# Issuing the packed keys' eight transfers from ScalarE instead of the SP queue

## The chip, the cores and the metric

The kernel runs on one core of one Trainium2 chip. The metric is the device time of one execution in microseconds (us), as the median of several runs. Beside it stands one profiled execution, whose trace is read here.

## The reference

The input x has 8 sequences of 2048 tokens with 256 features. One transformer layer is computed:

```
def attention(x):                       # 16 heads of 16
    k = q = heads(tanh(x))
    static = tanh(x) @ W.T
    v = heads(static)
    # per head, token by token:
    #   S = lam * S;  u = beta * (v_t - S^T k_t);  S += k_t u^T;  o_t = S^T q_t
    return layernorm(static + o) * gamma + beta_ln
x = layernorm(x + attention(x))
h = silu(x @ Wg.T) * (x @ Wu.T)         # 768 hidden features
return layernorm(x + h @ Wd.T)
```

The recurrence is sequential over the 2048 tokens, and the kernel works it in chunks.

## The kernel before, in words

The tokens are cut into 32 blocks of 64 tokens (8 sequences x 64 tokens), and each block into 4 chunks of 16 tokens, in which 8 x 16 = 128 rows fill the partitions. Within a chunk the recurrence becomes products with the chunk's gram matrix (keys by keys) and the inverse of a triangular matrix made from it. From chunk to chunk only the state S goes on.

The work is software-pipelined over steps numbered s. In step s the recurrence runs for block s, while block s+1 has its gram matrix and inverse computed, block s+2 has its input loaded, passed through tanh and transposed, and the two blocks behind go through the norms and the dense layers (gate, up, down). `p` is the parity of s. Each engine has a hand-written order of instructions for one step (`act_step`, `dve_step`, `pe_step`, `pool_step`, `sp_step`), and the engines are tied together by counting semaphores; `n_of(name, q)` is the count that stands for "block q is done". An engine's instructions start in their written order, so a wait holds back all that is behind it.

All transfers are issued by the queue of SyncE, the SP queue (`sp_step`, L1093). In one step its order is: `kb` part 0 (8 issues, L1073), the two stores of the transposed keys `xt` to `scr_x` in DRAM (L1004), the packed keys `xb` (8 issues, L1026), the block-diagonal keys `E` (8 issues, L1017; the profile names them `e`), the first store of the inverse (L1048), the residual (4 issues, L1083), the second store of the inverse (L1048), `tb` part 0 (8 issues, L1060), `kb` part 1 (8 issues), the gram matrix out to DRAM and back in head-major order (L1034, L1041), `tb` part 1 (8 issues), the next block's x (4 issues, L995) and the output (4 issues, L1091). Both `xb` and `E` are read from `scr_x`: the first packed, the second with each sequence's 16x16 pieces on a diagonal. TensorE multiplies them in `pe_gram` (L216) in the next step.

What ScalarE does around the place of the change, in `act_step`: the update of chunk 3 (L664), x1's high half 0 (L772), the decay (L673), x1's high half 1 (L772), the SiLU of gate tile 0 (`act_hidden`, L778), the scaled keys `k16` part 0 (L699), the high half of the inverse part 0 (`act_store_inverse`, L730), the product's high half (L784), gate tile 1 (L778) and the state's high half (L668). VectorE's order there is: 14 rounds of the inverse (L443, L451), `dve_multiply` for gate tile 0 (L495), the low half of the inverse part 0 (L458), the state (L388, L393, L399), and later, at the head of the next step, the low half of the inverse part 1 (L458 again).

Two more waits bear on the order: tanh of the next block (L677) waits for the load of x, and `act_static_out` (L706) waits for the output of an earlier block to have left its buffer.

Of the kernel before, what the change touches and what calls it, by code (L numbers as in the profile page):

```python
# [13 lines left out]
B, L, D = 8, 2048, 256  # L14
H, DH = 16, 16
# [20 lines left out]
def build(nc, x, W, ln_gamma, ln_beta, eta, lam_logit, w_gate, w_up, w_down, out):  # L36
# [3 lines left out]
    with ctx:  # L40
        def sb(name, shape, dt=F32):
            return ctx.enter_context(nc.sbuf_tensor(name, shape, dt))

        def sem(name):
            return ctx.enter_context(nc.semaphore(name))
# [28 lines left out]
        xb = sb("xb", [P, 2, H, C, NW], F16)  # L74
# [43 lines left out]
        scr_x = nc.dram_tensor("scr_x", [2, 2, P, B, T], F16).ap()  # L118
# [6 lines left out]
            xtd=32, e=128, xb=128, vp=2, v=2,  # L125
            gp=4, ga=4, g=4, gd=16, gh=16,
# [11 lines left out]
        SEM = {name: sem("s_" + name) for name in PER}  # L138
# [7 lines left out]
        s_hop = sem("s_hop")  # L146
# [6 lines left out]
        def n_of(name, q, k=None):  # L153

            k = PER[name] if k is None else k
            if k <= 0:
                q, k = q - 1, k + PER[name]
            return q * PER[name] + k if q >= 0 else 0
# [8 lines left out]
        def live(q):  # L167
            return 0 <= q < NS

        def later(q):  # L170
            return 1 <= q < NS
# [512 lines left out]
        def act_transpose_keys(act, q, p, half):  # L684
            src = pf[half][:, :].rearrange("p (n t) -> p t n", n=NW)
            dst = xt[:, half].rearrange("p z b i n -> p z (b i) n")
            act.wait_ge(SEM["xtp"], n_of("xtp", q, half + 1))
            if half == 0:
                act.wait_ge(SEM["vp"], n_of("vp", q - 1))
                act.wait_ge(SEM["xtd"], n_of("xtd", q - 1))  # L690
            act.activation(dst[:, 0], src, ACT.Copy, scale=KS).then_inc(SEM["xth"], 1)
# [75 lines left out]
        def act_transpose_x1(act, q, p, half):  # L767
            act.wait_ge(SEM["x1p"], n_of("x1p", q, half + 1))
            if half == 0:
                act.wait_ge(SEM["gt"], n_of("gt", q - 1))  # L770
                act.wait_ge(SEM["gu"], n_of("gu", q - 1))
            act.activation(x1hi[:, half, :], pg[half][:, :], ACT.Copy, scale=XS).then_inc(SEM["x1h"], 1)  # L772

        def act_hidden(act, q, p, t):
            k = t % 2
            act.wait_ge(SEM["gt"], n_of("gt", q, t + 1))
            act.wait_ge(SEM["hl"], n_of("hl", q, t - 1))
            act.activation(gate[:, k, :], pg[k][:, :], ACT.Silu, scale=W_SCALE / XS).then_inc(SEM["si"], 1)  # L778

        def act_multiply(act, q, p, t):  # L780
# [2 lines left out]
                act.wait_ge(SEM["dn"], n_of("dn", q - 1))  # L783
            act.activation(hhi[:, t, :], gate[:, t % 2, :], ACT.Copy).then_inc(SEM["hh"], 1)  # L784

        def act_step(act, s, p):
            if live(s):
                act_store_inverse(act, s, p, 1)
# [98 lines left out]
                act_decay(act, s, p, 3)  # L887
            if live(s - 1):
                act_transpose_x1(act, s - 1, 1 - p, 1)
                act_hidden(act, s - 1, 1 - p, 0)  # L890
            if live(s + 2):
                act_scale_keys(act, s + 2, p, 0)
# [104 lines left out]
        def sp_store_keys(sp, q, p, half):  # L997
            sp.wait_ge(SEM["xt"], n_of("xt", q, half + 1))
            sp.sem_inc(s_hop, 1)
            if half == 0:  # L1000
                sp.wait_ge(SEM["e"], n_of("e", q - 1))
                sp.sem_inc(s_hop, 1)
                sp.wait_ge(SEM["xb"], n_of("xb", q - 1))
            sp.dma_start(scr_x[:, half].rearrange("z p b t -> p z (b t)"),  # L1004
                         xt[:, half].rearrange("p z b i n -> p z (b i n)")).then_inc(SEM["xtd"], 16)
# [11 lines left out]
                sp.dma_start(E[p][DH * b:DH * (b + 1), :, :, b].rearrange("k z h i n -> k (z h) (i n)"),  # L1017
                             src[:, :, b, :]).then_inc(SEM["e"], 16)

        def sp_spread_packed_keys(sp, q, p):  # L1020
            src = scr_x.rearrange("z f (h k) b t -> k (z f h) b t", k=DH)
            sp.wait_ge(SEM["gp"], n_of("gp", q - 1))
            sp.sem_inc(s_hop, 1)
            sp.wait_ge(SEM["xtd"], n_of("xtd", q))
            for b in range(B):
                sp.dma_start(xb[DH * b:DH * (b + 1)].rearrange("k z h i n -> k (z h) (i n)"),  # L1026
                             src[:, :, b, :]).then_inc(SEM["xb"], 16)

        def sp_store_gram(sp, q, p):
            sp.wait_ge(SEM["g"], n_of("g", q))  # L1030
            sp.sem_inc(s_hop, 1)
            sp.wait_ge(SEM["gh"], n_of("gh", q - 1))

            sp.dma_start(scr_g.rearrange("h b i t -> (b i) h t"),  # L1034
                         gs[:, :, :, :].rearrange("p h j n -> p h (j n)")).then_inc(SEM["gd"], 16)
# [27 lines left out]
        def sp_load_kb(sp, q, p, g):  # L1063
            if q == 0:

                sp.wait_ge(s_pool0, 14)
                sp.sem_inc(s_hop, 1)
            sp.wait_ge(SEM["k16"], n_of("k16", q, g + 1))
            sp.sem_inc(s_hop, 1)
            sp.wait_ge(SEM["sp"], n_of("sp", q - 1, 2 * g + 2))  # L1070
            for b in range(B):
                rows = slice(C * b, C * (b + 1))
                sp.dma_start(kb[rows, g, :, b].rearrange("i h k z m -> i h (k z m)"),  # L1073
                             k16[rows, g].rearrange("i h k z m -> i h (k z m)")).then_inc(SEM[f"kb{g}"], 16)
# [18 lines left out]
        def sp_step(sp, s, p):  # L1093
            if live(s + 1):
                sp_load_kb(sp, s + 1, 1 - p, 0)
            if later(s + 2):
                sp_store_keys(sp, s + 2, p, 0)
                sp_store_keys(sp, s + 2, p, 1)
                sp_spread_packed_keys(sp, s + 2, p)
                sp_spread_keys(sp, s + 2, p)  # L1100
            if live(s + 1):
                sp_store_inverse(sp, s + 1, 1 - p, 0)
            if live(s):
                sp_load_residual(sp, s, p)
            if live(s + 1):
                sp_store_inverse(sp, s + 1, 1 - p, 1)
                sp_load_inverse(sp, s + 1, 1 - p, 0)
                sp_load_kb(sp, s + 1, 1 - p, 1)
            if live(s + 2):
                sp_store_gram(sp, s + 2, p)  # L1110
                sp_load_gram(sp, s + 2, p)
            if live(s + 1):
                sp_load_inverse(sp, s + 1, 1 - p, 1)
            if later(s + 3):
                sp_load_x(sp, s + 3, 1 - p)
            if live(s - 1):
                sp_store_out(sp, s - 1, 1 - p)


        def all_steps(eng, step):  # L1120
            for s in range(FIRST, LAST):
                step(eng, s, s % 2)
# [26 lines left out]
        @block.sync  # L1149
        def _(eng):  # L1150
            bc = lambda a, n: a.rearrange("(o n) -> o n", o=1).to_broadcast([P, n])
            sp_load_x(eng, 0, 0)
            eng.dma_start(sc[:, ETA:ETA + 1], eta.to_broadcast([P, 1])).then_inc(s_ldc, 16)
            eng.dma_start(sc[:, LOGIT:LOGIT + 1], lam_logit.to_broadcast([P, 1])).then_inc(s_ldc, 16)
            eng.dma_start(w_nat, W.rearrange("(a p) d -> p a d", p=P)).then_inc(s_ldw, 16)
            eng.dma_start(wg_nat, w_gate.rearrange("(t p) d -> p t d", p=P)).then_inc(s_ldn, 16)
            eng.dma_start(wu_nat, w_up.rearrange("(t p) d -> p t d", p=P)).then_inc(s_ldn, 16)
            for a in range(2):
                eng.dma_start(wd_nat[a], w_down[a * P:(a + 1) * P, :]).then_inc(s_ldn, 16)
            eng.dma_start(gamma[:, :], bc(ln_gamma, D)).then_inc(s_ldb, 16)  # L1160
            eng.dma_start(lnb[:, :], bc(ln_beta, D)).then_inc(s_ldb, 16)

            eng.wait_ge(s_pool0, 10)
            sp_store_keys(eng, 0, 0, 0)
            sp_store_keys(eng, 0, 0, 1)
            sp_spread_packed_keys(eng, 0, 0)
            sp_spread_keys(eng, 0, 0)
            all_steps(eng, sp_step)
            eng.wait_ge(SEM["out"], NS * PER["out"])
# [26 lines left out]
        @block.scalar  # L1196
        def _(eng):
            eng.wait_ge(s_ldc, 32)
            eng.activation(sc[:, OML:OML + 1], sc[:, LOGIT:LOGIT + 1], ACT.Sigmoid, scale=-1.0).then_inc(s_a0, 1)
            act_activate(eng, 0, 0)  # L1200
            act_transpose_keys(eng, 0, 0, 0)
            act_transpose_keys(eng, 0, 0, 1)
            for j, (_, dst) in enumerate(jobs):
                eng.wait_ge(s_ps, j + 1)
                eng.activation(dst, ps[j % 2], ACT.Copy).then_inc(s_wt, 1)
            eng.wait_ge(s_c, N_SETUP)
            all_steps(eng, act_step)
# [96 lines left out]
```

## Time and profile before

| | |
|---|---|
| Time, median of 3 runs | 1717.36 us |
| Lowest and highest | 1714.75 and 1728.76 us |
| Profiled execution: time | 1734.76 us |
| Profiled execution: span of the core | 1733.0 us |
| Mean granted TensorE clock (share of full speed) | 0.872 |
| Busy: TensorE, VectorE, ScalarE, GpSimd | 1373.0, 1359.0, 1118.9, 839.5 us |

The busy times are summed over the span of the one profiled execution. The SP queue is not counted as an engine in that table; its issues are seen in the timeline of the queue. In the timelines PE is TensorE, DVE VectorE, ACT ScalarE, POOL GpSimd, and SPq the queue of SyncE.

### The profile page before, as it was taken

Reading aid. Unit: us, or ns where it says so; the run is one execution under the profiler, and the core shown is the slowest. Engines: PE = TensorE matmul, PEld = TensorE weight load, DVE = VectorE, ACT = ScalarE, POOL = GpSimd, SP = SyncE. Lnnn points to the kernel's source line nnn. Section 1 sums busy time; section 2 is a strip of 40 time slices with the busy share of each in tenths; the row PEclk is TensorE's granted clock in tenths of the full one; section 3 lists DMA queues with packets and bytes.
Section 4 is the critical chain, followed back from the end, with each engine's and each line's share of the span. In section 5 each row is a group of like instructions: output and inputs, shape, how many; then the busy total and the mean of one; then the engine's idle time right before and its main releaser. Section 6 shows DMA issues by size and latency. Waiting matters only on the chain.

```text
span 1733.0 us, 53678 instructions
## 1 busy us (share of the span) xinstructions
PE 1373.0 (79%) x21032; PEld 1070.7 (62%) x21032; DVE 1359.0 (78%) x3461; ACT 1118.9 (65%) x2357; POOL 839.5 (48%) x1106
## 2 busy tenths in 40 slices
PE   4358778888887888878888888888888878888765
PEld 3346666666666666666666666666666666666532
DVE  4578888888888788888888888888888888888731
ACT  3336667666766767666776666766766666776543
POOL 6024455445444545444455554444555444455542
PEclk9558989888988999888999998989998898898866
DMA  4555544555554555555555665654555655555200
GB/s 119 116 106 119 111 114 114 117 118 111 130 111 116 113 123 117 117 119 118 116 121 118 118 121 112 124 116 114 123 120 108 115 119 117 116 120 109 57 13 25
DMA packets 701325, 190.98 MB, mean 110 GB/s; under 512 B 620944, under 2 KB 688528, under 8 KB 701072
## 3 DMA queue, kind: packets, MB, share of 16 engines
q1 hardware_dynamic: 701072, 187.56, 50.3%
q8 instruction: 165, 2.70, 0.7%
q14 instruction: 88, 0.72, 0.1%
HBM read 103.55 MB, written 67.11 MB: 98 GB/s over the span
## 4 chain that ended last, share of the span: by engine, by line
DVE 24%; SPq 22%; DMA 16%; PE 15%; issue 11%; ACT 8%; POOL 3%; ACTq 0%; POOLq 0%; DVEq 0%
SPq L1060 9%; DMA scr_g<-gs 6%; DMA xa<-L_attn_x 6%; PE pg L253 4%; SPq L1073 4%; PE pc L182 4%; DVE tt L451 4%; PE pu L253 4%; SPq L995 3%; DVE gs L443 3%; DVE gate L495 2%; DVE xt L406 2%; DVE x1lo L488 2%; DMA y_out<-v 2%; DVE U L382 2%
## 5 line engine op out<-in xcount | busy, mean ns | idle before, releaser
L954 POOL TENSOR_TENSOR hlo<-gate,hhi 128x512 f16<-128x512 f32 x192 | 263.7, 1383 | 377.3 <-ACT hhi L784 375.4
L182 PE MATMUL pc<-R,tb 128*128 128x32 f16 x4096 | 158.2, 186 | 128.1 <-DVE R L372 125.2
L182 PEld LDWEIGHTS pc<-R,tb 128*128 128x128 f16 x4096 | 146.7, 118 | 148.9 <-DVE R L372 145.7
L182 PE MATMUL pc<-U,kb 128*128 128x32 f16 x4096 | 158.9, 188 | 95.4 <-DVE U L382 95.3
L182 PEld LDWEIGHTS pc<-U,kb 128*128 128x128 f16 x4096 | 146.9, 118 | 124.7 <-DVE U L382 124.6
L182 PEld LDWEIGHTS pc<-S,e 128*128 128x128 f16 x4096 | 151.9, 118 | 61.7 <-DVE S L399 55.9
L182 PE MATMUL pc<-S,e 128*128 128x32 f16 x4096 | 157.3, 186 | 38.8 <-DVE S L399 38.7
L279 PE MATMUL pd<-wd_t,hhi 128*128 128x256 f16 x768 | 178.2, 278 | 7.9 <-POOL hlo L954 5.6
L279 PE MATMUL pd<-wd_t,hlo 128*128 128x256 f16 x768 | 178.0, 278 | 0.0
L216 PEld LDWEIGHTS pf<-xb,e 128*128 128x128 f16 x4096 | 153.6, 118 | 32.9 <-DMA e<-scr_x 17.6
L216 PE MATMUL pf<-xb,e 128*128 128x32 f16 x4096 | 156.2, 191 | 18.5 <-DMA e<-scr_x 16.9
L495 DVE SCALAR_TENSOR_TENSOR gate<-pu,gate 128x512 f32<-128x512 f32 x192 | 128.9, 685 | 49.9 <-ACT gate L778 34.9
L253 PE MATMUL pg<-x1hi,wg_t 128*128 128x512 f16 x384 | 155.0, 404 | 11.4 <-DVE x1lo L488 9.9
L443 DVE TENSOR_TENSOR gs<-tt,gh 128x56 f32<-128x56 f32 (+6 forms) x448 | 145.2, 324 | 23.6 <-ACT tt L720 14.6
L778 ACT ACTIVATE gate<-pg 128x512 f32<-128x512 f32 x192 | 114.0, 594 | 76.7 <-PE pg L253 73.7
L451 DVE TENSOR_TENSOR tt<-tt,gs 128x56 f32<-128x56 f32 (+6 forms) x448 | 152.3, 340 | 12.1
L253 PE MATMUL pg<-x1lo,wg_t 128*128 128x512 f16 x384 | 153.1, 399 | 0.0
L784 ACT ACTIVATE hhi<-gate 128x512 f16<-128x512 f32 x192 | 119.7, 629 | 50.4 <-DVE gate L495 49.0
L253 PE MATMUL pu<-x1hi,wu_t 128*128 128x512 f16 x384 | 149.1, 388 | 0.3 <-DVE gate L495 0.3
L253 PE MATMUL pu<-x1lo,wu_t 128*128 128x512 f16 x384 | 149.1, 388 | 0.0
L227 PE MATMUL pf<-w_t,xt 128*128 128x256 f16 x1024 | 140.1, 283 | 0.4 <-DVE gs L434 0.4
L434 DVE SCALAR_TENSOR_TENSOR gs<-pf,gs 128x256 f32<-128x256 f32 x128 | 84.9, 663 | 64.5 <-ACT gs L714 64.5
(134 smaller groups left out, 3229.0 us busy)
## 6 DMA issues: line engine op xcount, KB each, us to landing
xa<-L_attn_x SPq DMA_DIRECT2D x128, 128.0 KB
scr_x<-xt SPq DMA_DIRECT2D x64, 256.0 KB, 2.1
xb<-scr_x SPq DMA_DIRECT2D x256, 64.0 KB, 2.8
e<-scr_x SPq DMA_DIRECT2D x256, 64.0 KB, 3.5
scr_g<-gs SPq DMA_DIRECT2D x32, 512.0 KB, 3.5
gh<-scr_g SPq DMA_DIRECT2D x32, 512.0 KB, 3.4
kb<-k SPq DMA_DIRECT2D x512, 32.0 KB, 2.2
scr_t<-t SPq DMA_DIRECT2D x64, 256.0 KB, 3.5
```

The source lines that it names most:

```text
L182: last = pe.matmul(pc2[:, :, cols], stationary(h, a), moving[:, :, cols], start=a == 0, stop=a == 1)
L216: last = pe.matmul(pf[n % 2][:, 2 * h * C:2 * (h + 1) * C].rearrange("p (z j) -> p z j", z=2), E[p][:, ez, h, :, :, n].rearrange("p b i -> ...
L227: last = pe.matmul(pf[g][:, (n % 2) * D:(n % 2 + 1) * D], xt[:, half, xz, :, :, n].rearrange("p b i -> p (b i)"), w_t[:, half, wz, :], sta ...
L253: last = pe.matmul(bank[:, :], wt[:, half, t * P:(t + 1) * P], xp[:, half, :], start=half + part == 0, stop=half + part == 2)
L279: last = pe.matmul(pd[:, (n % 2) * D:(n % 2 + 1) * D], hp[:, t, n * P:(n + 1) * P], wd_t[:, t, :], start=n % 2 + t + part == 0, stop=n % 2 ...
L443: dve.tensor_tensor(tmp[:, m, 0:C - 1 - j, :], tt[:, m, j:j + 1, :].to_broadcast([P, j, C - 1 - j, NW]), gh[:, i, j, :][:, None].to_broadc ...
L451: dve.tensor_tensor(tt[:, m, i, :], tt[:, m, i, :], tmp[:, m, 0:C - 1 - j, :], ALU.add)\
L495: dve.scalar_tensor_tensor(gate[:, k, :], pu[k][:, :], W_SCALE * HS / XS, gate[:, k, :], ALU.mult, ALU.mult).then_inc(SEM["h"], 1)
L778: act.activation(gate[:, k, :], pg[k][:, :], ACT.Silu, scale=W_SCALE / XS).then_inc(SEM["si"], 1)
L784: act.activation(hhi[:, t, :], gate[:, t % 2, :], ACT.Copy).then_inc(SEM["hh"], 1)
L954: pool.tensor_tensor(hlo[:, t, :], gate[:, t % 2, :], hhi[:, t, :], ALU.subtract).then_inc(SEM["hl"], 1)
L1060: sp.dma_start(tb[C * b:C * (b + 1), g, :, b].rearrange("j h i z m -> j h (i z m)"), scr_t[g, :, b].rearrange("h j t -> j h t")).then_inc( ...
```

## The change

The eight issues of the packed keys leave the SP queue, together with the two waits ahead of them (`gp`: the gram products of the block before are done; `xtd`: the keys have landed in DRAM). The same eight issues, with the same two waits, now stand in ScalarE's order, behind x1's high half 1 and ahead of the SiLU of gate tile 0. For block 0 they stand in ScalarE's set-up, behind the two transposed keys. Transfers, sizes, counts and semaphores stay as they are.

```
+        def act_spread_packed_keys(act, q, p):
+            src = scr_x.rearrange("z f (h k) b t -> k (z f h) b t", k=DH)
+            act.wait_ge(SEM["gp"], n_of("gp", q - 1))
+            act.wait_ge(SEM["xtd"], n_of("xtd", q))
+            for b in range(B):
+                act.dma_start(xb[DH * b:DH * (b + 1)].rearrange("k z h i n -> k (z h) (i n)"),
+                              src[:, :, b, :]).then_inc(SEM["xb"], 16)
...
             if live(s - 1):
                 act_transpose_x1(act, s - 1, 1 - p, 1)
+            if later(s + 2):
+                act_spread_packed_keys(act, s + 2, p)
+            if live(s - 1):
                 act_hidden(act, s - 1, 1 - p, 0)
...
-        def sp_spread_packed_keys(sp, q, p):
-            src = scr_x.rearrange("z f (h k) b t -> k (z f h) b t", k=DH)
-            sp.wait_ge(SEM["gp"], n_of("gp", q - 1))
-            sp.sem_inc(s_hop, 1)
-            sp.wait_ge(SEM["xtd"], n_of("xtd", q))
-            for b in range(B):
-                sp.dma_start(xb[DH * b:DH * (b + 1)].rearrange("k z h i n -> k (z h) (i n)"),
-                             src[:, :, b, :]).then_inc(SEM["xb"], 16)
...
             if later(s + 2):
                 sp_store_keys(sp, s + 2, p, 0)
                 sp_store_keys(sp, s + 2, p, 1)
-                sp_spread_packed_keys(sp, s + 2, p)
                 sp_spread_keys(sp, s + 2, p)
...
             sp_store_keys(eng, 0, 0, 1)
-            sp_spread_packed_keys(eng, 0, 0)
             sp_spread_keys(eng, 0, 0)
...
             act_transpose_keys(eng, 0, 0, 1)
+            act_spread_packed_keys(eng, 0, 0)
             for j, (_, dst) in enumerate(jobs):
```

## Rows read from the trace of the kernel before

**Rows 1.** The page: busy time, and the chain of waits by engine and line.

```profile
PE 1373.0 (79%) x21032; PEld 1070.7 (62%) x21032; DVE 1359.0 (78%) x3461; ACT 1118.9 (65%) x2357; POOL 839.5 (48%) x1106
...
DVE 24%; SPq 22%; DMA 16%; PE 15%; issue 11%; ACT 8%; POOL 3%; ACTq 0%; POOLq 0%; DVEq 0%
SPq L1060 9%; DMA scr_g<-gs 6%; DMA xa<-L_attn_x 6%; PE pg L253 4%; SPq L1073 4%; PE pc L182 4%; DVE tt L451 4%; PE pu L253 4%; SPq L995 3%; DVE gs L443 3%; DVE gate L495 2%; DVE xt L406 2%; DVE x1lo L488 2%; DMA y_out<-v 2%; DVE U L382 2%
```

**Rows 2.** Timeline of the SP queue: start us, us taken, line, transfer and its count.

```profile
807.19 1.19 SPq L1004 DMA_DIRECT2D scr_x<-xt  x2
...
823.33 0.35 SPq L1048 DMA_DIRECT2D scr_t<-t  x1
...
842.35 2.66 SPq L995 DMA_DIRECT2D xa<-L_attn_x  x4
...
854.89 1.19 SPq L1004 DMA_DIRECT2D scr_x<-xt  x2
857.81 4.02 SPq L1026 DMA_DIRECT2D xb<-scr_x  x8
862.28 4.88 SPq L1017 DMA_DIRECT2D e<-scr_x  x8
867.28 0.41 SPq L1048 DMA_DIRECT2D scr_t<-t  x1
867.74 2.65 SPq L1083 DMA_DIRECT2D res<-L_attn_x  x4
871.04 0.34 SPq L1048 DMA_DIRECT2D scr_t<-t  x1
871.50 5.60 SPq L1060 DMA_DIRECT2D tb<-scr_t  x8
877.22 5.95 SPq L1073 DMA_DIRECT2D kb<-k  x8
883.29 0.53 SPq L1034 DMA_DIRECT2D scr_g<-gs  x1
...
891.21 2.67 SPq L995 DMA_DIRECT2D xa<-L_attn_x  x4
...
903.97 1.56 SPq L1004 DMA_DIRECT2D scr_x<-xt  x2
```

**Rows 3.** Timeline of ScalarE behind x1's high halves: start us, us taken, [idle before, releaser].

```profile
860.31 0.59 ACT L772 ACTIVATE x1hi<-pg 128x512 f16<-128x512 f32 x1
862.75 0.60 ACT L778 ACTIVATE gate<-pg 128x512 f32<-128x512 f32 x1 [1.85 <-PE pg L253]
863.25 0.83 ACT L699 ACTIVATE k<-xa,kcol 128x512 f16<-128x512 f32 x1
864.87 0.69 ACT L730 ACTIVATE t<-tt 128x512 f16<-128x512 f32 x1 [0.80 <-DVE tt L451]
```

**Rows 4.** Timeline of VectorE in the same step.

```profile
865.59 0.69 DVE L458 SCALAR_TENSOR_TENSOR t<-tt,t 128x512 f16<-128x512 f32 x1 [0.15 <-ACT t L730]
866.20 0.48 DVE L388 SCALAR_TENSOR_TENSOR Sp<-pc,sc,S 128x256 f32<-128x256 f32 x1
...
870.27 0.68 DVE L458 SCALAR_TENSOR_TENSOR t<-tt,t 128x512 f16<-128x512 f32 x1
```

**Rows 5.** The line that issues the packed keys: min/median/max ns of one issue.

```profile
L1026 SPq DMA_DIRECT2D xb<-scr_x x256: 309/486/1984, 17.9 to 1561.9; - x128
```

**Rows 6.** Timeline of the SP queue: the longest group of the packed keys' eight issues.

```profile
106.53 5.52 SPq L1026 DMA_DIRECT2D xb<-scr_x  x8
```

**Rows 7.** The page's DMA issues: KB each, median us from issue to landing.

```profile
xb<-scr_x SPq DMA_DIRECT2D x256, 64.0 KB, 2.8
```

**Rows 8.** Timeline of TensorE: the first gram product of the next step.

```profile
871.39 2.29 PE L216 MATMUL pf<-xb,e 128*128 128x32 f16 x64
```

**Rows 9.** Waits of the SP queue: us in total, times, longest us.

```profile
SPq L1046 <- DVE t L458: 38.0, 29, 13.5
```

**Rows 10.** Waits of ScalarE: us in total, times, longest us.

```profile
ACT xa L677 <- DMA xa<-L_attn_x: 30.7, 25, 2.2
```

## The prediction

> **What bounds the kernel now.** Read the page's chain of waits first [rows 1]. By engine it is mixed: VectorE 24%, the SP queue 22%, transfers 16%, TensorE 15%, ScalarE 8%. No engine is saturated (the busiest is at 79%), so the bound is a loop through several of them, and the time of one step is what has to be read. By line, the SP queue's largest parts are L1060 and L1073, the inverse and the scaled keys; the packed keys' own line is not among those shown.
>
> Next, the timeline of the SP queue, where one step goes from one store of the transposed keys (L1004) to the next [rows 2]. The step at 854.89 took 903.97 - 854.89 = 49.1 us, the one before it 47.7. Over the 30 steps from 56.73 us on the mean is 50.0 (46.9 to 51.6). What sets it is seen where the next x is loaded (L995): 842.35 - 807.19 = 35.2 us into the short step, 891.21 - 854.89 = 36.3 us into the other. Over the 28 steps with all their transfers the next step starts 12.5 to 13.9 us behind that load, which leads through tanh (ScalarE waited for the load 25 times [rows 10]), the transposes and xt back to L1004. So the loop is: xt, then compute until the inverse's second store (L1048), then the SP queue alone until x is loaded, then tanh and transposes.
>
> The question for this change is which part of that loop it touches. It frees the SP queue ahead of the second store. There the queue isn't late: VectorE ends the low half it stores at 870.27 + 0.68 = 870.95 [rows 4], the store starts at 871.04 [rows 2]. I took the same difference in all 30 steps: 0.08 to 0.10 us in 24, 0.14, 0.27, 0.44 and 0.46 in four, 1.34 and 1.71 in the first two, in the start-up. Stores of the inverse waited for VectorE 38.0 us in all [rows 9]. Behind the second store the queue is the bound, and the change removes nothing there. In front of it the bound is compute, VectorE with ScalarE in between: this is the part to which the change adds.
>
> **Removed from the SP queue.** Eight issues, 4.02 us in this step [rows 2], up to 5.52 [rows 6]. The keys E then start at 857.8 instead of 862.3, the first store of the inverse waits for VectorE's 865.59 + 0.69 = 866.28 [rows 4] instead of going out at 867.28, the residual follows 1.0 us earlier, and the second store waits for 870.95 as before. The gain is what the 30 differences hold above the usual 0.09: 0.05 + 0.18 + 0.35 + 0.37 in steady steps and 1.25 + 1.62 at the start, 3.8 us; I take 4. Behind it late comes VectorE, at once.
>
> **Added to ScalarE.** The two waits first. The gram products of the block before are long done. The keys' landing in DRAM was what the SP queue waited for until 857.81, and ScalarE comes there at 860.3 to 860.9, so this wait costs nothing in a steady step; with no dense work yet, in the start-up, ScalarE will wait but has nothing urgent behind it. Then eight issues. The trace of before has none on ScalarE, so their price has to be bounded. One issue took 309 ns at least and 486 ns in the median on the SP queue [rows 5], and one group of eight 4.02 us [rows 2] to 5.52 [rows 6], 4.55 in the mean of 30. The same descriptors have to be written whoever asks for them; I take 4.55 (the mean, as ScalarE gets its share of the long issues), with 8 x 0.309 + 7 x 0.05 between them = 2.8 us as the low end. Where do they start? ScalarE starts the second high half at 860.31 and ends it at 860.90 [rows 3]; the issues could start anywhere between. So they end between 860.31 + 4.02 = 864.33 and 860.90 + 5.52 = 866.42, and most likely at about 860.6 + 4.55 = 865.15.
>
> What is queued behind them: the SiLU of gate tile 0 (it starts at 862.75), the scaled keys (862.75 + 0.50, 0.83 long), and the high half of the inverse, which starts at 864.87 because VectorE's last round of the inverse ends then (idle before it 0.80 us [rows 3]). From the end of the issues to that high half are 0.50 + 0.82 = 1.32 us, so ScalarE has slack until 864.87 - 1.32 = 863.55. The issues end 0.8, 1.6 or 2.9 us behind that. Who waits: VectorE's low half (865.59), and behind it in VectorE's order the state of chunk 3 at 866.20 [rows 4], the statistics, the scaled keys, two products of the gate and the second low half, which is what the SP queue waits for. From 865.59 to the second low half at 870.27 VectorE has no idle time that could make up for it. On TensorE, gate tile 3 waits for the SiLU of tile 1, which is behind all of this on ScalarE, and slides by the same amount. The delay therefore goes round the loop in full: 1.6 us in each of the 29 steps that have dense work behind the place (s = 1 to 29), 46 us; ends 29 x 0.8 = 23 and 29 x 2.9 = 84 us.
>
> **Moved: the packed keys themselves.** They land 2.8 us after their issue [rows 7], so at about 868 instead of 864.7. The gram product needs them at 871.39 [rows 8]. With 3.4 us to spare this costs nothing; with issues to 866.42 it is 2.2 us. E, which was the later of the two, comes 4 us earlier.
>
> On the page, the Trainium skill bears on this at one place. In *DMA: Bandwidth & Descriptors*, section "Issuing engines are not separate DMA queues", it says that issuing from several engines saves only the sequencer's time to issue. That speaks against the change: here that time is saved on a queue that then waits, and it is paid on an engine in the loop; no run so far shows transfers issued by ScalarE.
>
> **Sum.** 46 - 4 = +42 us, against the profiled execution 1734.76 + 42 = 1777 us. The profiled execution is 1% above the median of the runs, 1717.36, and the steps are the same in both as far as one can see, so the forecast for the median is 1717.4 + 42 = 1759; I say 1758 us. The mechanism's own range is 1717 - 4 + 23 = 1736 to 1717 - 4 + 84 = 1797 us.
>
> **Rival 1, the two issuers hinder each other: slower still.** In the new order the SP queue issues E from 857.8 to about 861.8, and ScalarE begins at 860.3. If only one of them can be served at a time, ScalarE's issues end up to 861.8 - 860.3 = 1.5 us later: 3.1 us per step, 90 us, 1717 - 4 + 90 = 1803 us. For it: issues on the SP queue come in a steady 0.49 us, which looks like a unit at work and not like a sequencer. Against: E's last three or four issues are the only ones that overlap. Chance 15%. The skill's page *Perfetto Trace Analysis*, section "DMA Instruction — HWDGE (DVE, Sync)", states that the descriptor generator is locked for one issuer at a time and that the wait for the lock lies inside the profiled time; by it this rival would be the forecast, and no trace of before shows it.
>
> **Rival 2, ScalarE's idle time covers the issues: no change.** ScalarE sits idle 1.85 us in front of the SiLU [rows 3], and 0.80 in front of the inverse's high half. Issues that end by 863.55 cost nothing. From 860.31 that leaves 3.24 us, 0.405 us for each with the gap; the shortest of before would make it (2.8 us). The time is then 1717 - 4 = 1713 us. It decides at the mean issue: below 0.40 us no change, above it the forecast. Against it: only the first issue of a group was that short in the step I looked at. Chance 18%.
>
> **Rival 3, a lighter SP queue is a faster one.** From the second store to the load of x the queue took 842.35 - 823.33 = 19.0 us in the short step [rows 2], and 20.4 in the mean of 28 (36.9 us into the step less 16.5). The difference comes from single issues of 1.2 to 2.0 us (1984 ns is the longest [rows 5]) and from a late landing of the gram matrix. If these come from the number of transfers the queue has in hand, eight of 57 fewer issues per step could remove them: at most 1.4 x 30 = 42 us. With half of it, and rival 2 true, 1717 - 4 - 21 = 1692 us. The point is at the issues between L1060 and L995: they must become shorter, and ScalarE's must fit in its idle time. Against it: the stretch has the same 30 issues as before, and the eight leave another stretch. Chance 8%.
>
> That the change doesn't do what it says would mean that ScalarE waits for the keys' landing in each step and not only in the start-up; with 2.5 us to spare I give it 3%.
>
> **How the numbers follow.** Forecast 56%, rival 1 15%, rival 2 18%, rival 3 8%, the last 3% on the slow side. A measurement of this kernel can tell about 1% from no change: the three runs lie 0.8% apart. Faster by over 1% is rival 3, 8%; within 1% (1700 to 1735) rival 2 and the forecast's lowest edge, 20%; slower the rest, 72%. The range takes in the forecast's ends, rival 1 just about and rival 2's 1713: 1711 to 1804 us.
>
> **What the profile will show.** Right: eight issues of `xb` on ScalarE's queue of about 0.49 us each behind L772; idle time in front of L778 there gone; L730 some 1.6 us later against xt's store; the SP queue waiting 3 to 5 us more in front of the two stores of the inverse, yet with the load of x 38 us or more into the step; steps of 51.5 us in the mean. Wrong: issues under 0.40 us or beside running activations (rival 2), issues of 0.7 us and more while E is issued (rival 1), a stretch from L1048 to L995 shorter than 19.5 us (rival 3). A gram product that waits for `xb` would be a cost that I haven't counted, and so would a lower granted clock in the dense work, where TensorE would now pause.

## The result, and the profile after

The changed kernel takes 1785.8 us (median; before 1718.1), a ratio of 1.039 with a 95% interval of 1.036 to 1.042: 67.7 us slower. The profiled execution of after took 1782.1 us, that of before 1734.8. The profiled one of before was slower than any other run of it (1714.8 to 1728.8), so the difference of the two traces, 47 us, is less than that of the medians; the medians decide.

The page of after: busy times, the transfer queues (packets, MB, share of the 16 transfer engines), and the chain of waits. They answer to [rows 1].

```profile
span 1780.3 us, 53678 instructions
PE 1386.0 (78%) x21032; PEld 1067.3 (60%) x21032; DVE 1363.5 (77%) x3461; ACT 1115.4 (63%) x2357; POOL 840.9 (47%) x1106
...
q1 hardware_dynamic: 565904, 170.76, 43.7%
q10 hardware_dynamic: 135168, 16.79, 11.9%
...
DVE 20%; SPq 18%; PE 13%; DMA 13%; issue 12%; ACT 12%; ACTq 9%; POOL 3%; POOLq 0%; DVEq 0%
SPq L1062 9%; ACTq L791 9%; PE pc L182 6%; DMA scr_g<-gs 5%; SPq L1075 5%; DMA xa<-L_attn_x 4%; DVE gate L495 3%; SPq L1006 3%; DVE xt L406 2%; DMA y_out<-v 2%; PE pg L247 2%; ACT x1hi L772 2%; PE pf L239 1%; DVE Sp L366 1%; ACT v L735 1%
```

The transfers of `xb` are now in a queue of their own (q10). In the chain there is a member that was not there before, ScalarE's queue, with 9% of the span, all of it line 791, the eight issues. The engines' busy times have hardly moved (TensorE 1386.0 us instead of 1373.0, the others by under 5 us): nothing computes much longer, the chain has become longer. The lines behind the new function have moved: in after, L1004 is L1015, L1017 is L1028, L1048 is L1050, L1060 is L1062, L1073 is L1075, L1034 is L1036 and L995 is L1006.

One step of the SP queue, in the columns of [rows 2]:

```profile
878.83 1.19 SPq L1015 DMA_DIRECT2D scr_x<-xt  x2
881.81 4.02 SPq L1028 DMA_DIRECT2D e<-scr_x  x8
894.01 0.34 SPq L1050 DMA_DIRECT2D scr_t<-t  x1
...
898.68 0.35 SPq L1050 DMA_DIRECT2D scr_t<-t  x1
...
919.48 2.65 SPq L1006 DMA_DIRECT2D xa<-L_attn_x  x4
...
931.47 1.63 SPq L1015 DMA_DIRECT2D scr_x<-xt  x2
```

The step took 931.47 - 878.83 = 52.6 us. E goes out right behind the keys' stores. Then the queue waits for 8 us: the first store of the inverse starts 15.2 us into the step (before 867.28 - 854.89 = 12.4 [rows 2]), the second 19.9 us (16.15), the load of x 40.7 us (36.3). All that the queue gained it spends on waiting for VectorE, and then some:

```profile
SPq L1048 <- DVE t L458: 247.3, 64, 13.1
```

(the queue's waits in us in total, times, longest), which was 38.0 us in 29 times [rows 9]. And the same step on ScalarE, in the columns of [rows 3]:

```profile
884.24 0.59 ACT L772 ACTIVATE x1hi<-pg 128x512 f16<-128x512 f32 x1
884.26 6.96 ACTq L791 DMA_DIRECT2D xb<-scr_x  x8
891.32 0.60 ACT L778 ACTIVATE gate<-pg 128x512 f32<-128x512 f32 x1 [6.50 <-issue]
...
892.54 0.66 ACT L730 ACTIVATE t<-tt 128x512 f16<-128x512 f32 x1
```

The eight issues begin with the second high half, not behind it, and take 6.96 us, until 891.22. The SiLU of gate tile 0 starts at 891.32, 7.1 us behind the high half's start (2.4 before [rows 3]), and the inverse's high half follows 1.2 us later without any idle time. The waits of the engines say the same (us in total, times, longest):

```profile
ACT gate L778 <- issue: 115.1, 22, 6.6
...
PE pg L253 <- ACT gate L778: 43.4, 46, 2.8
```

ScalarE stood 115 us in front of L778 without a semaphore to wait for ("issue": its queue was busy with transfers), and TensorE waited 43 us for SiLUs of L778, which was 1.5 us, once, in before. ScalarE's idle time there until TensorE's product is done was 73.7 us in before and is 37.9 now; with the 115 us it has grown by some 80 us.

From here on I use means over the 28 steps that have all transfers and dense work. Each is taken from the timelines, in us behind the first store of the keys of its step:

| kernel | issues on ScalarE, first to last | inverse's high half (L730) starts | second store of the inverse | load of x | step | median, us |
|---|---|---|---|---|---|---|
| before | - | 10.17 | 16.51 | 36.93 | 50.14 | 1718 |
| after | 5.61 to 11.24 | 12.62 | 18.78 | 38.96 | 51.83 | 1786 |

Read along the row, the delay of 2.45 us at L730 is 2.27 at the second store, 2.03 at the load of x and 1.69 in the step. The last gives the difference of the two traces (28 x 1.69 = 47 us), less than that of the medians. What makes the delay shrink on its way isn't shown.

### The profile page after: what moved, and what is told of

Its sections match the earlier page's. It is cut to its first block, busy times and chain, and to the rows that moved or that the text cites. A ratio compares the mean times of both kernels' runs of the same rounds, so it can differ in the third digit from the quotient of the medians.

```text
span 1780.3 us, 53678 instructions
## 1 busy us (share of the span) xinstructions
PE 1386.0 (78%) x21032; PEld 1067.3 (60%) x21032; DVE 1363.5 (77%) x3461; ACT 1115.4 (63%) x2357; POOL 840.9 (47%) x1106
## 4 chain that ended last, share of the span: by engine, by line
DVE 20%; SPq 18%; PE 13%; DMA 13%; issue 12%; ACT 12%; ACTq 9%; POOL 3%; POOLq 0%; DVEq 0%
SPq L1062 9%; ACTq L791 9%; PE pc L182 6%; DMA scr_g<-gs 5%; SPq L1075 5%; DMA xa<-L_attn_x 4%; DVE gate L495 3%; SPq L1006 3%; DVE xt L406 2%; DMA y_out<-v 2%; PE pg L247 2%; ACT x1hi L772 2%; PE pf L239 1%; DVE Sp L366 1%; ACT v L735 1%
## 5 line engine op out<-in xcount | busy, mean ns | idle before, releaser
L778 ACT ACTIVATE gate<-pg 128x512 f32<-128x512 f32 x192 | 113.6, 592 | 156.8 <-issue 115.1
L279 PE MATMUL pd<-wd_t,hhi 128*128 128x256 f16 x768 | 174.5, 274 | 7.4 <-POOL hlo L965 5.0
L216 PEld LDWEIGHTS pf<-xb,e 128*128 128x128 f16 x4096 | 153.7, 118 | 34.9 <-DMA e<-scr_x 19.5
L279 PE MATMUL pd<-wd_t,hlo 128*128 128x256 f16 x768 | 174.1, 274 | 0.0
```

The source lines that it names most:

```text
L216: last = pe.matmul(pf[n % 2][:, 2 * h * C:2 * (h + 1) * C].rearrange("p (z j) -> p z j", z=2), E[p][:, ez, h, :, :, n].rearrange("p b i -> ...
L279: last = pe.matmul(pd[:, (n % 2) * D:(n % 2 + 1) * D], hp[:, t, n * P:(n + 1) * P], wd_t[:, t, :], start=n % 2 + t + part == 0, stop=n % 2 ...
```

## The experiments

The kernel before was measured again beside the experiments. Its median was 1721.5 us beside half of the issues, ten copies and the two kernels without E, and 1720.1 us beside six copies, half of E's bytes and the two kernels with the exchange. Each is compared with its own.

### Half of the issues

```
in act_spread_packed_keys:       for b in range(4):       ... act.dma_start(xb[...])
in sp_step, ahead of E, again:   for b in range(4, B):    ... sp.dma_start(xb[...])
```

> Four of the packed keys' eight transfers (sequences 0 to 3) are issued by ScalarE at the new place, four (4 to 7) by the SP queue at the old place. Theory (ScalarE is held by its issues, with some 3.1 us of slack before anybody waits): four issues hold it 4 x 0.51 = 2.1 us, inside the slack, so the time is that of the kernel before, 1710 to 1722 us. Rival (the cost comes with each transfer that goes through the second queue, by contention with the first): about half of the change's 67 us, 1750 us.

Measured: 1723.4 us, ratio 1.004 (1.000 to 1.007). One step of ScalarE, as above:

```profile
799.80 1.96 ACTq L791 DMA_DIRECT2D xb<-scr_x  x4
802.22 0.60 ACT L778 ACTIVATE gate<-pg 128x512 f32<-128x512 f32 x1 [1.85 <-PE pg L253]
...
804.34 0.68 ACT L730 ACTIVATE t<-tt 128x512 f16<-128x512 f32 x1 [0.80 <-DVE tt L451]
```

Four issues fit into the time in which ScalarE waits for TensorE's gate product anyway (the SiLU starts 2.42 us behind the issues' start, with the same 1.85 us of idle time as before, and the 0.80 us in front of L730 are there too). In the mean L730 starts at 10.16 us, as in before. The median is 1 us above the range that I gave and 1.9 us above before's (by the interval 0.3 to 11.5 us), far from the rival's 1750. So the rival is out: transfers that go through the second queue cost next to nothing as such. Nor does the SP queue's relief by four issues buy anything: the second store starts at 16.50 us instead of 16.51.

This kernel shows one thing more. All sixteen issues are out after 8.4 us here (3.30 to 11.69 us into the step) instead of 9.2, and the last of them are E's, by the SP queue. The last two issues of E now take 1.18 and 1.06 us in the mean (0.51 in before), and E's group 6.07 us instead of 4.49. So the long issues go with whoever issues last, not with ScalarE. On the SP queue they are free, as it would wait for VectorE anyway.

### ScalarE held without any transfer

```
 act_transpose_x1(act, s - 1, 1 - p, 1)
+for i in range(10):                      # 6 in the second kernel
+    act.wait_ge(s_dump, 10 * (s - 1) + i)
+    act.activation(dump[:, :], gamma[:, :], ACT.Copy).then_inc(s_dump, 1)
 act_hidden(act, s - 1, 1 - p, 0)
```

All of it on top of the kernel before, with `xb` on the SP queue. Ten copies:

> The kernel before, with all transfers on the SP queue, and ten copies of 128x256 elements into an unused buffer on ScalarE at the place of the change, each waiting for the one before: some 5 us of ScalarE held, no transfer moved. Theory (the time ScalarE is held at this place is the whole cost): the high half of the inverse starts 12 to 12.8 us into the step instead of 10.2, and the time is 1775 to 1800 us, as in the changed kernel at the same hold. Rival (contention of two queues carries a large part): clearly less, 1740 to 1755 us, at the same hold.

Six copies:

> As the run with ten copies, with six: ScalarE is held some 2.6 us at the place of the change, all transfers on the SP queue. Theory (slack until 8.8 us into the step, then every us counts): the hold ends at about 8.7 us, the high half of the inverse starts at 10.2 us as before, and the time is that of the kernel before, 1715 to 1727 us. Rival (what counts is how long ScalarE is held, without a threshold): six tenths of the 39 us of ten copies, 1740 to 1748 us.

Ten copies: 1760.7 us, ratio 1.025 (1.021 to 1.028). Six copies: 1721.8 us, 1.001 (0.9995 to 1.0025). The ten in one step of ScalarE:

```profile
824.71 0.59 ACT L774 ACTIVATE x1hi<-pg 128x512 f16<-128x512 f32 x1
825.18 4.45 ACT L894 ACTIVATE dump<-gamma 128x256 f32<-128x256 f32 x10
829.54 0.58 ACT L780 ACTIVATE gate<-pg 128x512 f32<-128x512 f32 x1
...
830.75 0.65 ACT L732 ACTIVATE t<-tt 128x512 f16<-128x512 f32 x1
```

A copy takes 0.44 us, so the ten hold ScalarE for 4.45 us, shorter than I meant, in the mean until 10.55 us into the step; the SiLU starts in the mean at 10.50 and L730 at 11.71, 1.54 us late. The time falls below the range I gave because the hold did. Set against the delay it is what the theory wants: 39 us for 1.54 us, 25 us for each. With six, the SiLU starts at 8.74 us, L730 at 10.17 as before, and nothing is lost. So there is a threshold between the two. Worked out, it is a SiLU that starts at 10.17 less the 1.22 us from SiLU to L730 (12.62 - 11.40 in after): 8.95 us into the step.

### Without the transfers of E

```
-for b in range(B):
-    sp.dma_start(E[p][...], src[:, :, b, :]).then_inc(SEM["e"], 16)
```

and the two waits on `e`, once in the kernel before and once in the changed one. The kernel before without E:

> The kernel before without the eight transfers of the block-diagonal keys E and the waits on them; the gram products and the products with the state read E as it was cleared at the start, so the output is not the layer's. It is the reference point for the next kernel. The E transfers end ahead of the second store of the inverse, which waits for VectorE, so both theories expect little: 1705 to 1718 us.

The changed kernel without E:

> The changed kernel without the eight transfers of E and the waits on them (E stays cleared). Theory (ScalarE's issues lengthen to 5.6 us for eight because the transfer engines are still busy with E): the group of eight shrinks to 4.1 to 4.3 us, one us over the slack, so 29 x 1.0 = 29 us above the same kernel with the SP queue issuing: 1735 to 1745 us. Rival (issues from ScalarE are long by themselves, or because of its own ring): group still 5.6 us, 60 us or more above the other: about 1775 us.

Measured: 1717.1 us with `xb` on the SP queue (ratio 0.997, 0.995 to 1.000) and 1749.2 with `xb` on ScalarE (1.018, 1.014 to 1.021), 32 us apart where with E they are 67 apart. Two neighbouring groups of issues of the second, by ScalarE:

```profile
813.60 4.07 ACTq L790 DMA_DIRECT2D xb<-scr_x  x8
...
863.77 5.02 ACTq L790 DMA_DIRECT2D xb<-scr_x  x8
```

These two take 4.07 and 5.02 us; in the mean they run from 5.68 to 10.21 us into the step, 4.53 us against 5.63 with E. L730 is 11.59 - 10.24 = 1.35 us late instead of 2.45. The group is longer than the 4.1 to 4.3 us that I expected, and the time 4 us above its range, but the rival's 5.6 us and 1775 are out. So half of the loss hangs on E being in transfer at the same time. The first kernel also bounds what eight issues are worth on the SP queue at this place: 4 us in all, with an interval that reaches nearly to nothing, and E's bytes and the waits on them are gone with them. Its second store starts at 16.53 us in the mean, no earlier than before's 16.51. In the start-up it does gain: the step that starts at 151.61 us in before starts at 145.36.

### E with half the bytes in the same eight issues

```
-sp.dma_start(E[p][rows, :, :, b] ..., src[:, :, b, :])
+sp.dma_start(E[p][rows, 0, :, b] ..., src[:, 0:H, b, :])
```

> The changed kernel with each of E's eight transfers cut to the high parts of the keys: the same eight issues by the SP queue, half the bytes and half the pieces; the low parts of E stay cleared, so the output is less exact than the layer's. Theory (ScalarE's last issues lengthen because the transfer engines are behind with E's pieces): its group of eight falls from 5.6 to 4.6 to 5.1 us, and the time to 1755 to 1772 us. Rival (it is the two issuers at once that lengthen them): the group stays at 5.6 us and the time at 1780 to 1788 us.

Measured: 1749.7 us, ratio 1.017 (1.015 to 1.020). This line in the changed kernel (min/median/max ns of one issue; then the landing in us):

```profile
L791 ACTq DMA_DIRECT2D xb<-scr_x x256: 309/508/2602, 18.2 to 1616.7; - x128
...
DMA to landing us min/median/max: 3.0/5.0/10.8
```

and with half of E:

```profile
L791 ACTq DMA_DIRECT2D xb<-scr_x x256: 309/507/1975, 18.9 to 1587.9; - x128
...
DMA to landing us min/median/max: 2.3/3.2/7.5
```

The median of an issue is the same, 507 and 508 ns; what goes is the long tail and the late landing, 5.0 us back to 3.2. The group takes 4.55 us in the mean, as without E at all, while the SP queue still makes its eight issues at the same time. So it isn't the second issuer that lengthens ScalarE's issues but the transfers that are not yet worked off. (The bytes and the number of pieces are both halved here; which of them counts isn't shown.) Group and time (5 us) both came out just below my ranges.

### The SP queue's own stretch, shortened

```
 sp_store_gram(sp, s + 2, p)
-sp_load_gram(sp, s + 2, p)            # stays here for s < 0
 sp_load_inverse(sp, s + 1, 1 - p, 1)
+sp_load_gram(sp, s + 2, p)
```

In the kernel before:

> The kernel before with one exchange in the SP queue's order: the eight issues of the inverse's part 1 stand between the gram matrix's store and its load, in the 3.5 us in which the queue waits for that store to land, and no longer behind the load. Theory (the loop is bound by the SP queue from the second store of the inverse to the load of x): x is loaded some 2.5 us earlier, until VectorE's sums of squares bound it, steps fall from 50.1 to about 48, and the time to 1650 to 1680 us. Rival (compute bounds the step, and the queue's late load is hidden): within 10 us of 1720.

In the changed kernel:

> The same exchange in the changed kernel. Theory (the hold of ScalarE and the queue's stretch lie one behind the other in the loop): the exchange gives as much here, and the two kernels with it lie 55 to 70 us apart, this one at 1710 to 1745 us. Rival (the two are beside each other, so that the loop without the queue's delay has room for ScalarE's): less than 30 us apart.

Measured: 1689.7 us, ratio 0.982 (0.979 to 0.984), and 1748.6 us, 1.017 (1.014 to 1.019). One step of the SP queue in the first, in the columns of [rows 2], then its chain of waits by engine and two of the queue's waits:

```profile
836.67 1.18 SPq L1004 DMA_DIRECT2D scr_x<-xt  x2
...
864.39 0.54 SPq L1034 DMA_DIRECT2D scr_g<-gs  x1
865.05 4.40 SPq L1060 DMA_DIRECT2D tb<-scr_t  x8
869.57 0.38 SPq L1041 DMA_DIRECT2D gh<-scr_g  x1
871.73 3.24 SPq L995 DMA_DIRECT2D xa<-L_attn_x  x4
...
885.24 1.18 SPq L1004 DMA_DIRECT2D scr_x<-xt  x2
```

```profile
DVE 33%; PE 24%; issue 16%; ACT 13%; POOL 8%; SPq 3%; DMA 2%; POOLq 0%; DVEq 0%; ACTq 0%
```

```profile
SPq L995 <- DVE nb L418: 32.6, 27, 1.8
...
SPq L1039 <- DMA scr_g<-gs: 5.8, 2, 2.9
```

The eight issues of the inverse's part 1 now fill the time in which the queue waited 108.5 us in 32 times for the gram matrix to land (now 5.8 us in 2). The SP queue's share of the chain falls from 22% [rows 1] to 3%. x is loaded 35.3 us into the step in the mean, not the 34.4 I expected: at the load the queue now waits for VectorE's sums of squares, 27 times, so compute is the next bound, and the step takes 48.83 us. The gain, 30 us, is less than the 40 to 70 us that my range stood for; the range was missed by 10 us. It is the fastest kernel of this study.

With the change on top, 59 us are lost again, within the 55 to 70 expected, though the time itself is 4 us above its range, since the gain was smaller. L730 is 12.45 - 9.99 = 2.46 us late, as in the plain pair. The stretch that holds ScalarE and the stretch of the SP queue lie one behind the other in the loop; taking one away leaves most of the price of the other (59 of 67 us).

### All of them together

| pair | L730 later by, us | time, us | us for each us |
|---|---|---|---|
| six copies, before | 0.00 | 1.7 | |
| four issues, before | -0.01 | 1.9 | |
| xb on ScalarE, on the SP queue, both without E | 1.35 | 32.1 | 24 |
| xb on ScalarE with half of E, before | 1.36 | 29.6 | 22 |
| ten copies, before | 1.54 | 39.2 | 25 |
| after, before | 2.45 | 67.7 | 28 |
| the same two with the queue's exchange | 2.46 | 58.9 | 24 |

Whatever holds ScalarE, copies or issues, and whatever the transfers do, the loss follows the start of L730, at 22 to 28 us for each us. The delay occurs in 29 steps, so 29 would be the whole of it passed on, and the four other pairs pass on 22 to 25. In the traces too the delay shrinks on its way: of the ten copies' 1.54 us, 1.21 are left at the load of x and 1.08 in the step, of the last pair's 2.46 us 1.89 and 1.86. That the plain pair lies highest I can't account for; a few us of it are within the spread of the runs.

## Why the prediction was right, point by point

The forecast was 1758 us, by a sum of +42. The measured 1785.8 us lie inside the range, in the direction forecast, and for the forecast's reason: ScalarE is held beyond its slack. But they lie nearer to rival 1's 1803 us than to the forecast, and 26 of the 67.7 us of loss were missed.

**The loop and its bounds: right in the steady steps.** The gain from the SP queue was put at 4 us, and everything behind the second store at nothing. Four issues fewer moved that store by 0.01 us; without E's eight it moved by 0.02, and the run was 4 us faster. The exchange of the queue's order showed that the stretch behind the store was a bound, as read from the 12.5 to 13.9 us between the load of x and the next step.

**The start-up: wrong, by a few us.** 2.9 of the 4 us of gain were to come from the first steps, where ScalarE was said to have nothing urgent behind the issues. In the step that starts at 56.7 us there is no SiLU, but the scaled keys and the inverse's high half are queued behind them all the same: the issues hold ScalarE from 59.64 to 65.57 us, and L730 starts at 66.72 us instead of 64.06. The next step starts at 105.69 us instead of 103.59, a loss of 2.1 us and no gain.

**The slack of ScalarE: right.** The prediction had it end at 863.55, 8.7 us into the step; six copies end at 8.62 us in the mean and cost nothing, and the SiLU's edge, 8.95 us less the 0.16 us from the end of the issues to the SiLU in after, puts it at 8.8.

**The start of the issues: right, at its early end.** I took a point between the start and the end of the second high half. They begin with its start (884.24 and 884.26), 0.3 us earlier than the sum had it. In 29 steps that takes 8 us off the sum.

**The length of the group: the mis-sized term.** "I take 4.55 (the mean, as ScalarE gets its share of the long issues)" was 5.63 us, and in single steps 6.96 and 7.06 where my upper end was 5.52. The difference of 1.1 us, 31 us in 29 steps, is most of what was missing: 42 + 31 - 8 = 65 us against 67 measured. The price was read off one queue that issues all sixteen transfers one behind the other: in before they go out from 3.24 to 12.39 us into the step, in 9.15 us, with 4.5 us for either group. In after two queues overlap, and all sixteen are out from 3.37 to 11.24 us, in 7.87. The transfer engines have to work off the same bytes sooner, and who comes later, ScalarE, waits for them; E's own group stays at 4.46 us. Without E the group on ScalarE is 4.53 us, the value I took.

**"Goes round the loop in full": not borne out.** The sum takes each us of delay as 29 us of time. The four other pairs gave 22 to 25, by which the 2.45 us would have cost 54 to 61. That 65 meets 67 so well is therefore in part luck. The start-up's 5 us are not in that sum either. The steps were forecast at 51.5 us in the mean and came out at 51.83, though L730 was 2.45 us late instead of the 1.6 forecast: only 1.69 us of it reached the step in these two traces.

**Rival 1, the two issuers hinder each other: half of its price was seen, its reason wasn't.** I said that only one might be served at a time. Single issues in the step shown, from both queues:

```profile
884.29 0.49 SPq L1028 DMA_DIRECT2D e<-scr_x  x1
884.65 0.51 ACTq L791 DMA_DIRECT2D xb<-scr_x  x1
...
885.35 0.49 SPq L1028 DMA_DIRECT2D e<-scr_x  x1
...
886.27 0.51 ACTq L791 DMA_DIRECT2D xb<-scr_x  x1
886.81 0.59 ACTq L791 DMA_DIRECT2D xb<-scr_x  x1
887.43 1.16 ACTq L791 DMA_DIRECT2D xb<-scr_x  x1
888.62 2.60 ACTq L791 DMA_DIRECT2D xb<-scr_x  x1
```

The two queues issue beside each other, one each in about half a us, at 0.51 and 0.49 us: together they are twice as fast as one. Over 29 steps 141 of ScalarE's issues overlap with one of E's; their median is 0.51 us, the same as in the kernel without E. The Trainium skill's page *Perfetto Trace Analysis*, section "DMA Instruction — HWDGE (DVE, Sync)", has the generator locked for one issuer at a time and the wait inside the profiled time; these rows show no such wait. Long are the last issues only, 1.16 and 2.60 us, when E's have been out for over a us; of the 49 that took over 0.9 us in those steps, 42 overlap with no issue of E. What they meet is seen in the windows (columns as headed; the next to last is the transfer engines' share, which adds up the times of their packets and passes 1 where several are in hand at once). First after, then the same part of the step in before:

```profile
core 0: us, PE busy (x) PEld busy (x) DVE busy (x) ACT busy (x) POOL busy (x), PEclk, DMA share, GB/s
884.00:886.00 2.00, 1.72 (x35) 1.36 (x35) 1.97 (x6) 0.83 (x2) 0.00 (x0) 0.72 1.02 132
886.00:888.00 2.00, 2.00 (x11) 0.89 (x10) 1.80 (x6) 0.00 (x0) 0.00 (x0) 1.00 1.64 99
888.00:890.00 2.00, 1.23 (x6) 0.39 (x4) 0.70 (x3) 0.00 (x0) 0.00 (x0) 1.00 1.65 118
890.00:892.00 2.00, 0.03 (x1) 0.03 (x2) 0.05 (x1) 0.68 (x2) 0.00 (x0) 0.98 1.03 82
892.00:894.00 2.00, 2.00 (x5) 0.71 (x6) 1.41 (x3) 2.00 (x4) 0.21 (x1) 0.50 0.22 30
```

```profile
860.00:862.00 2.00, 1.71 (x36) 1.35 (x35) 1.97 (x6) 0.90 (x3) 0.00 (x0) 0.89 0.77 122
862.00:864.00 2.00, 2.00 (x11) 0.89 (x10) 1.83 (x6) 1.25 (x2) 0.00 (x0) 1.00 0.73 120
864.00:866.00 2.00, 2.00 (x11) 0.88 (x9) 1.75 (x6) 1.20 (x3) 0.00 (x0) 1.00 0.53 81
```

The share rises from 1.02 to 1.64 and 1.65 just when the issues get long, while what is moved stays at before's level (99 and 118 GB/s; 81 to 122 in before's three rows, with a share of 0.53 to 0.77); and half the bytes with the same issues took the tail away. So it is the backlog of the transfers that the second issuer's extra rate builds up, and it has a second price on the last lines: TensorE ran dry from 890 to 892 and got 0.50 of its clock, the 1.2 GHz level, from 892 to 894, where before had the full 2.4 GHz at that point of the step. How much of the 67 us that is I haven't separated; over the span the granted clock is the same, 0.871 against 0.872.

**Rivals 2 and 3: out.** The shortest issue was 309 ns on ScalarE as well, but as the first of a group; the mean was 0.7 us. The SP queue's stretch did not fall under the 19.5 us of rival 3's sign: 38.96 - 18.78 = 20.2 us from the second store to the load of x, 20.4 before. (That rival counts 57 issues in a step of the SP queue; the trace has 66, and 58 in after.)

**The packed keys' landing: free, as said, with less to spare.** They land 5.0 us after their issue instead of 2.8 [rows 7]. The gram products, delayed themselves, didn't wait for them: the last packed keys were there at least 1.9 us ahead of the first product, 5.8 in before.

## What to carry to other kernels

A transfer that moves to another engine's queue takes that engine for the length of its issues, here 0.5 us each and up to 2.6 when earlier transfers are still being worked off. Look for the idle time in front of the next instruction that somebody waits for, and move only as many issues as fit (four were free, eight cost 67 us). Before that, ask whether the queue that gets rid of them is the bound at that place: it had been waiting for VectorE there, and the place where it was the bound, some 20 us later, could be mended by filling one of its own waits, for a gain of 30 us.

## What the runs showed of the hardware that I had not expected

Issues from SyncE's and ScalarE's queues ran at the same time at 0.49 and 0.51 us each, without slowing each other. An issue's length depends on the transfers in flight ahead of it, and not on its own bytes alone: the same eight took 5.63 us in the mean behind all of E, 4.55 behind half of it and 4.53 without it. The long ones fall to the queue that issues last: with half of the issues on each queue they were the SP queue's. An issue on ScalarE starts while the activation ahead of it still runs (884.26 against 884.24 to 884.83).
